# A Perceiver layer on one core: query, key and value weights split inside the walk, three second products in three passes, a residual on GpSimd

## What is computed

```python
x = x + xattn(layernorm(x), ctx)          # x 128 x 512, ctx 12544 x 512, 16 heads
# k' = relu(k Wkf'), v: kv = sum over ctx of k' v, ksum = sum of k';  out = (q' kv) / (q' ksum) @ Wo'
x = x + attn(layernorm(x))
# q, k, v = rms(x) @ w_qkv.T;  y = sigmoid(rms q) * cumsum(exp(rms k) * v) / cumsum(exp(rms k))
# u, g = split(y @ w_swiglu.T)            # 2048 each
# attn(x) = x + (u * silu(g)) @ w_out.T   # the "x +" here adds the normed input once more
x = x + ffn(layernorm(x))                 # 2 experts, top-1, hidden 2048, squared leaky relu
```

## Time and profile before

| | |
|---|---|
| median of 3 runs | 875.67 us (875.64 to 875.98) |
| the profiled execution's own time | 875.99 us |
| its span in the profile | 874.2 us |
| from one full tile to the next, and from one short tile to the next | 7.42 us (693.65 to 701.07), 6.12 us (726.83 to 732.95) |
| granted TensorE clock | 1.00 over the whole span |
| busy: TensorE, VectorE, ScalarE, GpSimd | 861.8, 668.1, 563.6, 363.1 us |

### The profile page before, as it was taken

How to read it: one execution, slowest core, us unless ns; L and a number is a source line. 1 busy time by engine, 2 the same in 40 slices (tenths; PEclk the granted TensorE clock), 3 DMA queues, 4 the chain that set the end, 5 groups by cost and what they waited for, 6 DMA issues and landing times.

```text
span 874.2 us, 14769 instructions
## 1 busy us (share of the span) xinstructions
PE 861.8 (99%) x4728; PEld 742.4 (85%) x4728; DVE 668.1 (76%) x1048; ACT 563.6 (64%) x988; POOL 363.1 (42%) x208
## 2 busy tenths in 40 slices
PE   8999999999999999999999999999999999899998
PEld 6888888888888888888888888888888888778788
DVE  5777777777777777777777777777777788889586
ACT  5666666666666666666666666666666666754453
POOL 2654454445555444555554444445555433000000
PEclk9999999999999999999999999999999999999999
DMA  7212121121101010101010101001010000659740
GB/s 267 95 52 88 58 72 72 61 83 50 70 24 48 24 48 24 48 24 48 24 48 24 48 24 42 30 28 44 24 48 25 25 1 28 241 202 354 250 157 13
DMA packets 18504, 64.15 MB, mean 73 GB/s; under 512 B 2224, under 2 KB 2992, under 8 KB 18096
## 3 DMA queue, kind: packets, MB, share of 16 engines
q1 hardware_dynamic: 17760, 63.58, 20.6%
q10 hardware_dynamic: 720, 0.25, 0.1%
HBM read 63.56 MB, written 0.26 MB: 73 GB/s over the span
## 4 chain that ended last, share of the span: by engine, by line
PE 95%; ACT 2%; DVE 1%; DMA 1%; issue 0%; SPq 0%; DVEq 0%; ACTq 0%
PE kv_ps L798 11%; PE f_ps L785 10%; PE v_bank L701 10%; PE k_bank L701 10%; PE v_bank L702 10%; PE k_bank L702 10%; PE v_bank L703 10%; PE k_bank L703 10%; PE kv_ps L1016 3%; PE kv_ps L1035 2%; ACT w_hi L594 1%; PE k_bank L881 1%; PE v_bank L881 1%; PE k_bank L887 1%; PE v_bank L893 1%; PE v_bank L887 1%
## 5 line engine op out<-in xcount | busy, mean ns | idle before, releaser
L412 POOL TENSOR_TENSOR ksum_acc<-ksum_acc,kf 128x1024 f32<-128x1024 f32 x96 | 230.9, 2405 | 190.0 <-DVE kf L1137 190.0
L500 ACT ACTIVATE fb<-f_ps 128x256 f32<-128x256 f32 x392 | 149.6, 382 | 172.5 <-PE f_ps L785 165.2
L1130 DVE TENSOR_TENSOR kf<-f_ps,fb 128x256 f32<-128x256 f32 x392 | 165.5, 423 | 109.0 <-ACT fb L500 103.5
L405 POOL TENSOR_TENSOR ctx_lo<-ctx_raw,ctx_hi 128x512 fp32r<-128x512 f32 x92 | 119.5, 1299 | 170.1 <-ACT ctx_hi L475 170.1
L785 PEld LDWEIGHTS f_ps<-bd,keys 128*128 128x128 f32 x784 | 146.3, 188 | 33.8 <-issue 1.3
L785 PE MATMUL f_ps<-bd,keys 128*128 128x256 f32 x784 | 155.9, 281 | 1.3 <-DVE kf L1130 1.3
L701 PE MATMUL k_bank<-ctx_hi,wk_lo 128*128 128x512 f32 (+1 forms) x392 | 152.5, 389 | 0.8 <-DVE ctx_lo L1209 0.7
L701 PE MATMUL v_bank<-wv_hi,ctx_lo 128*128 128x512 f32 x388 | 153.2, 395 | 0.0
L483 ACT ACTIVATE keys<-k_bank,bias_cols 64x512 fp32r<-64x512 f32 (+1 forms) x194 | 131.0, 675 | 34.4 <-PE k_bank L703 31.9
L702 PE MATMUL v_bank<-wv_lo,ctx_hi 128*128 128x512 f32 x388 | 152.6, 393 | 0.0
L702 PE MATMUL k_bank<-ctx_lo,wk_hi 128*128 128x512 f32 (+1 forms) x392 | 152.2, 388 | 0.0
(11 more groups left out here) (214 smaller groups left out, 935.4 us busy)
## 6 DMA issues: line engine op xcount, KB each, us to landing
ctx_raw<-in_ctx SPq DMA_DIRECT2D x46, 512.0 KB, 3.3
early<-in_stream SPq DMA_DIRECT2D x14, 1024.0 KB, 4.9
raw<-in_stream SPq DMA_DIRECT2D x10, 1024.0 KB, 5.3
early<-in_stream SPq DMA_DIRECT2D x14, 512.0 KB, 4.3
early<-in_ctx SPq DMA_DIRECT2D x2, 512.0 KB, 6.3
early<-in_wv SPq DMA_DIRECT2D x1, 1024.0 KB, 8.7
early<-in_wq SPq DMA_DIRECT2D x1, 1024.0 KB, 10.7
w_o<-in_wo SPq DMA_DIRECT2D x1, 1024.0 KB, 5.3
```

Of the source, the lines that this page charges most:

```text
L405: pool.tensor_tensor(ctx_lo[:, s, :, cols], raw[:, :, t % 2 * P:(t % 2 + 1) * P], ctx_hi[:, s, :, cols].bitcast(f32), ALU.subtract).then_i ...
L412: pool.tensor_tensor(ksum_acc[:, :].rearrange("p (j f) -> p j f", f=P), ksum_acc[:, :].rearrange("p (j f) -> p j f", f=P), kf[:, t % 2, :, ...
L500: act.activation(fb[:, i % 2, :, :], f_ps[i % 2][:, :].rearrange("p (j x f) -> p j x f", j=2, x=2) [:, :, 1, :], ACT.Copy).then_inc(fb_rea ...
L1130: dve.tensor_tensor(kf[:, t % 2, 2 * i:2 * i + 2, :], f_ps[i % 2][:, :].rearrange("p (j x f) -> p j x f", j=2, x=2)[:, :, 0, :], fb[:, i % ...
```

## The change

Four things. The parts of GK, GQ and GV are made in the last twelve tiles before `tile_last`: ScalarE copies a quarter of a group (128 x 512) at the end of each tile, and VectorE subtracts the quarter before at the start of the next one, ahead of share 0. For that their high parts get places of their own (`w_lo[0..2]`), four groups instead of seven are loaded in the walk, and the loads behind it begin with group 4. Second, GD[0], GD[1] and GD[2] are made in three passes, with their weights and hidden values split. Third, the residual with the normed input is made by GpSimd, ahead of the gated layer. Fourth, the lists of splits behind the walk are shifted accordingly.

```diff
-NG_EARLY = 7
+NG_EARLY = 4
+SLOTS_EARLY = 7
...
-SPLIT = [GK, GQ, GV, GG[0], GU[0], GG[1], GU[1], GG[2], GU[2], GG[3], GU[3], *GF_[0:6], GP[3],
+BEFORE = [GK, GQ, GV]
+SPLIT = [GG[0], GU[0], GG[1], GU[1], GG[2], GD[0], GU[2], GG[3], GU[3], GD[1], GD[2], *GF_[0:6], GP[3],
          GF_[6], GP[4], GF_[7], *GP[5:8]]
...
+DOWNS = [0, 1, 2, *range(DFF // D + FIRST, 3 * DFF // D)]
+
+
+def slot_of(g):
+    return (g + 3) % RAWS
...
         def high(g):
-            return w_hi[SPLIT.index(g) % HIS]
+            return w_lo[g] if g in BEFORE else w_hi[SPLIT.index(g) % HIS]
...
@@ block.sync
             sp.wait_ge(f_done, JOBS * NT)
-            load_group(7)
-            load_group(8)
+            load_group(4)
+            load_group(5)
 
             sp.wait_ge(kv_done, NT + 1)
             sp.wait_ge(ksumT_done, 1)
-            load_group(9)
-            load_group(10)
-
-            for g in range(RAWS, NG):
-                sp.wait_ge(group_used, g - RAWS + 1)
+            load_group(6)
+            load_group(7)
+
+            for g in range(8, NG):
+
+                sp.wait_ge(group_used, min(g - 7, 3) if g < 14 else g - 10)
                 load_group(g)
...
@@ block.gpsimd
+            z1 = gate[:, 0, :]
+            pool.wait_ge(act_ready, 4)
+            pool.tensor_scalar(z1, x1[:, :], stat[:, 6:7], stat[:, 8:9], ALU.subtract, ALU.mult).then_inc(z1_ready, 1)
+            pool.wait_ge(z1_ready, 1)
+            pool.tensor_tensor(x1[:, :], x1[:, :], z1, ALU.add).then_inc(x1_ready, 1)
             rstd(3, 8, 1)
...
@@ block.scalar
+            def qkv_high(i):
+                g, k = BEFORE[i // KC], i % KC
+                act.activation(high(g)[:, k, :], raw(g)[:, k, :], ACT.Copy).then_inc(qkv_hi_ready, 1)
+
+            def period(c, s, splits=TILES, keys=CHUNK, pieces=0):
                 n = TILES * c
                 for t in range(TILES):
                     tile(n + t, t, keys=((c + 1, 1 - s, t, k_bank, keys),),
                          splits=((2 * c + 4 + t // 2, s, t),) if t < splits else ())
+                    if pieces:
+                        qkv_high(TILES * (pieces - 1) + t)
...
-            period(LAST - 3, 1)
-            period(LAST - 2, 0, splits=LAST_TILES)
-            period(LAST - 1, 1, splits=0, keys=HALF)
+            act.wait_ge(early_loaded, 16 * NPIECE)
+            period(LAST - 3, 1, pieces=1)
+            period(LAST - 2, 0, splits=LAST_TILES, pieces=2)
+            period(LAST - 1, 1, splits=0, keys=HALF, pieces=3)
...
             act.wait_ge(f_done, JOBS * NT)
-            for g in (2, 3, 4):
-                weight_high(g)
+            weight_high(GU[0])
+            weight_high(GG[1])
 
             act.wait_ge(kv_done, NT + 1)
-            for g in (5, 6):
-                weight_high(g)
+            weight_high(GU[1])
...
-                t = hid_hi[n % 2][:, :, :] if n >= DFF // D + FIRST else hid_T2[n % 2]
+                t = hid_hi[n % 2][:, :, :] if n in DOWNS else hid_T2[n % 2]
...
@@ block.tensor
                     group(GG[n], k_ps[n % 2], 0 if n else 3)
                     if n == 2:
-                        hidden_down(0, GD[0], True, False)
+                        hidden_down_split(0, GD[0], True, False)
                     group(GU[n], v_ps[n % 2])
                 if 1 <= n <= nd:
                     hidden_turn(n - 1)
-                if n >= 3:
-                    hidden_down(n - 2, GD[n - 2], False, n == nd + 1)
+                if n in (3, 4):
+                    hidden_down_split(n - 2, GD[n - 2], False, False)
+            hidden_down(nd - 1, GD[nd - 1], False, True)
...
@@ block.vector
+            def qkv_low(i):
+                g, k = BEFORE[i // KC], i % KC
+                dve.wait_ge(qkv_hi_ready, i + 1)
+                dve.tensor_tensor(low(g)[:, k, :], raw(g)[:, k, :], high(g)[:, k, :].bitcast(f32), ALU.subtract)\
+                   .then_inc(qkv_lo_ready, 1)
+
+            def period(c, s, keys=CHUNK, pieces=0):
                 n = TILES * c
                 for t in range(TILES):
+                    i = TILES * (pieces - 1) + t
+                    if pieces and i:
+                        qkv_low(i - 1)
                     tile(n + t, t, keys=((c + 1, 1 - s, t, k_bank, keys),))
...
-            period(LAST - 3, 1)
-            period(LAST - 2, 0)
-            period(LAST - 1, 1, keys=HALF)
+            period(LAST - 3, 1, pieces=1)
+            period(LAST - 2, 0, pieces=2)
+            period(LAST - 1, 1, keys=HALF, pieces=3)
+            qkv_low(3 * KC - 1)
...
+            before_gate = ((7, 10), (10, 13), (13, 16), (18, 20))
+            before_up = ((), (), (16, 18), (20, 21))
+            dve.wait_ge(x1_ready, 1)
             for n in range(nd):
+                low_pieces(*before_gate[n])
 
                 dve.wait_ge(gateg_ready, n + 1)
                 e = gate[:, n % 2, :]
                 link(dve.tensor_tensor(e, k_ps[n % 2], e, ALU.mult))
+                if before_up[n]:
+                    low_pieces(*before_up[n])
                 dve.wait_ge(group_used, GU[n] + 1)
                 dve.tensor_tensor(hid[:, n % 2, :], v_ps[n % 2], e, ALU.mult).then_inc(hid_ready, 1)
-                low_pieces(14 + 4 * n - 2 * (n == 3), 18 + 4 * n - 2 * (n >= 2))
-                if n == 2:
-
-                    dve.wait_ge(rstd_ready, 2)
-                    link(dve.tensor_scalar(eq[:, :], x1[:, :], stat[:, 6:7], stat[:, 8:9], ALU.subtract, ALU.mult))
-                    link(dve.tensor_tensor(x1[:, :], x1[:, :], eq[:, :], ALU.add))
+                if n:
+                    hidden_low(n - 1)
+            low_pieces(21, 26)
```

More of the change, by code:

```diff
@@ L66, in perceiver_kernel @@
         scope.close()
-        w_lo = [sb(f"w_lo{i}", [P, KC, D], f32r) for i in range(NG_EARLY)]
+        w_lo = [sb(f"w_lo{i}", [P, KC, D], f32r) for i in range(SLOTS_EARLY)]
         x_sb = sb("x_sb", [P, D])
@@ L536, in tile_last @@
                 features_share(n, 3, False)
-            def period(c, s, splits=TILES, keys=CHUNK):
+            def qkv_high(i):
+                g, k = BEFORE[i // KC], i % KC
+                act.activation(high(g)[:, k, :], raw(g)[:, k, :], ACT.Copy).then_inc(qkv_hi_ready, 1)
+            def period(c, s, splits=TILES, keys=CHUNK, pieces=0):
                 n = TILES * c
@@ L671, in _ @@
                     act.wait_ge(hid_ready, n - 1)
+                if n == 0:
+                    act.wait_ge(x1_ready, 1)
                 act.activation(gate[:, n % 2, :], k_ps[n % 2], ACT.Sigmoid).then_inc(gateg_ready, 1)
+                for g in ((GU[2], GG[3]), (), GD[2:3], GF_[1:2])[n]:
+                    weight_high(g)
                 if n:
                     hidden_turned(n - 1)
-                for g in (GU[3:4], GF_[0:1], GF_[1:2], GF_[2:4])[n]:
+                for g in ((), (GU[3], GD[1]), GF_[0:1], ())[n]:
                     weight_high(g)
             hidden_turned(nd - 1)
+            for g in GF_[2:4]:
+                weight_high(g)
             turned_high(4)
@@ L872, in wait_low, with wait_high @@
             def wait_low(g, h):
-                pe.wait_ge(w_lo_ready, PIECES.index((g, h)) + 1)
+                if g in BEFORE:
+                    pe.wait_ge(qkv_lo_ready, KC * BEFORE.index(g) + 2 * h + 2)
+                else:
+                    pe.wait_ge(w_lo_ready, PIECES.index((g, h)) + 1)
+            def wait_high(g):
+                if g in BEFORE:
+                    pe.wait_ge(qkv_hi_ready, KC * BEFORE.index(g) + KC)
+                else:
+                    pe.wait_ge(w_hi_ready, 2 * SPLIT.index(g) + 2)
             def hi_hi(g, ps, x, cols, start, turned=0):
-                pe.wait_ge(w_hi_ready, 2 * SPLIT.index(g) + 2)
+                wait_high(g)
                 for k in range(KC):
@@ L1020, in hidden_down, with hidden_down_split @@
                 last.then_inc(group_used, 1)
-            def hidden_down_split(n, g, last_one):
-                i = n - DFF // D - FIRST
+            def hidden_down_split(n, g, first, last_one):
+                i = DOWNS.index(n)
                 pe.wait_ge(hidT_ready, n + 1)
-                pe.wait_ge(w_hi_ready, 2 * SPLIT.index(g) + 2)
+                wait_high(g)
                 for bs in ([[0], [1]] if last_one else [[0, 1]]):
@@ L1035, in hidden_down_split @@
                                 last = pe.matmul(half_ps[b], x[n % 2][:, k, :], w[:, k, b * D // 2:(b + 1) * D // 2],
-                                                 start=False, stop=last_one and x is hid_lo and k == KC - 1)
+                                                 start=first and x is hid_hi and not low_w and k == 0,
+                                                 stop=last_one and x is hid_lo and k == KC - 1)
                     if bs == [0]:
@@ L1041, in _ @@
             nd = DFF // D
-            for n in range(nd + 2):
+            for n in range(nd + 1):
                 if n < nd:
@@ L1188, in tile_last @@
                     masked_features(n, t)
```

(18 more changed lines are left out.)

59 lines of the change are left out of this document (27 added, 32 removed).

## The result

| | before | after |
|---|---|---|
| median, 7 runs each | 875.90 us (875.46 to 877.27) | 878.86 us (878.51 to 879.97) |
| profiled execution, its span | 875.99, 874.2 us | 878.68, 876.2 us |

The changed kernel is slower: ratio 1.0031, interval 1.0021 to 1.0041. That is 2.96 us where 2.0 were forecast. Some executions of either kernel show a mean granted clock of 0.998 instead of 1.00 and take 1 to 2 us longer; the medians include them.

A forecast was written before the change was run, and what follows sets the result against it. TensorE, busy 99% of the span, was taken to bound the kernel. The terms, -0.50 - 1.86 + 0.1 + 4.3 = +2.0 us, put the median at 877.7 us, with the range 874.7 to 878.9.

The forecast's parts named there:

- Quarters on VectorE in the walk: In short tiles, the subtraction ahead of share 0 waits for GpSimd's feature sum and delays share 1; 4.3 us lost.
- the next instruction starts 0.08 before its record ends: After the held quarter on VectorE, share 0 starts 0.08 us before the quarter's recorded end, at K + 2.92.
- Pricing a short tile by the lateness of share 1: Share 1 starts 0.93 us late, TensorE's job 3 and the next keys with it, so each such tile pays 0.93.
- the full hold: Main case: the walk's subtraction stands still until GpSimd's sum is done, less 0.14; 876.5 to 878.7 us, chance 0.62.
- The first (not held, 873.4): The walk's subtraction finds VectorE idle and isn't held up, so only the gains stay; 873.4 us, chance 0.14.
- The second, half speed: Subtraction and GpSimd's sum share the port at half speed, quarter 1.2 us, 1.4 lost; 874.8 us, chance 0.17.
- A hold that breaks early: The walk's subtraction is held only for a part of GpSimd's sum; up to 876.4 us, within the half-speed chance of 0.17.
- The third: Longer hold costs seven full tiles 0.1 to 0.2 each, residual on GpSimd meets VectorE's products for 0.5; 879.2, chance 0.07.
- Backlog: Behind the walk, fewer half groups on ScalarE let the first copy of turned_high(2) start earlier; 0.50 us gained.
- Three passes: In the gated layer, three second products on TensorE take 2.84 us each instead of 3.46; 1.86 us gained.
- ScalarE's quarters: In the walk, each quarter copy of about 0.5 us fits ScalarE's idle time ahead of share 0; nothing lost.
- The residual: Two GpSimd instructions near 772 end by about 774.5 and could hold one VectorE product 0 to 0.2; 0.1 lost.

The follow-up runs named there:

- the first two runs: Changed kernel with the walk's VectorE subtractions replaced by one-operand bn_stats, 873.67 us; changed kernel with GpSimd's feature sum in short tiles cut to 8 columns, 873.89 us.
- The version with full tiles: Changed kernel with the twelve quarters moved one period earlier into the last twelve full tiles, on VectorE ahead of share 3; 873.49 us, ratio 0.9965.

## Why the prediction was right in sign and short by one

**Quarters on VectorE in the walk: forecast 4.3, measured 5.05. The mechanism was right, the size off.** The hold was as forecast: the quarter got through 0.14 before GpSimd's end and ended 0.55 after it (forecast 0.5), and took 1.97 (near 2.0). Full tiles kept their length (708.40 - 700.99 = 7.41). The step that failed is "the next instruction starts 0.08 before its record ends": share 0 starts 0.03 after the quarter's end (725.85 against 725.82), so shares 0 and 1 came at K + 3.03 and K + 4.50, where 2.92 and 4.39 were forecast. That is 0.11 in each of five tiles, 0.55 of the missing 0.75. By the starts of the keys before and after, the five tiles lose 0.83, 1.05, 1.06, 1.05 and 1.06, together 5.05 (to job 3 at 742.25 against 737.51, plus 0.31 by which this execution's walk ran earlier from its start-up). Most of the rest, about 0.1, is in the first of them. The forecast said 0.6 for the first and 0.93 for the others. Pricing a short tile by the lateness of share 1 was sound: share 1 is 4.50 - 3.46 = 1.04 late and the tile 1.06 longer, over the path that the prediction named. The idle stands elsewhere than I wrote: not 0.9 ahead of job 3, but 0.31 ahead of job 2 and 0.26 ahead of job 3. Job 2 needs share 0, which the prediction had end at K + 3.34; in a short tile job 2 is due at 730.41 - 727.37 = K + 3.04, so by its own numbers job 2 had to wait. I had looked at job 2 in full tiles only.

The range held by 0.04 (878.86, with 878.9 as its end), and the 876.5 to 878.7 that I gave to the full hold itself did not. The mechanism is shown; that the number fell inside is luck.

**Rivals.** The first (not held, 873.4) is what the first two runs make by hand, 873.67 and 873.89, so its time was right and its condition false. The second, half speed, is out: at half speed 0.68 becomes 1.36 at most, and it took 1.97. A hold that breaks early is out as well, since the quarter ends where GpSimd's end puts it. The third needed a hold longer than in the rows, which no run shows.

The Trainium skill's rule that speaks against this place (SBUF — State Buffer, "Who interferes with whom") is borne out on both sides. With two SBUF inputs the instruction is held, 1.97 against 0.68. The page also says that a VectorE instruction with at most one SBUF input, outside certain modes, does not contend; the run with one operand agrees, with 0.69 beside GpSimd's sum. One SBUF tile is not safe in every case, though: the `tensor_scalar` at 754.09 reads only `den` and still ended with GpSimd's instruction. No run here takes that case apart.

**Backlog: 0.50 forecast, 0.50 measured**: the copy starts 0.48 behind the transposes instead of 0.98. **Three passes: 1.86 forecast, 1.87 measured** from the first product of the gated layer to the end of the last (782.89 to 818.99 against 778.65 to 816.62); no low part came late, and each takes 2.86 rather than 2.84. **ScalarE's quarters** cost nothing, as forecast. **The residual: 0.1 forecast, 0 seen in the trace.** Its instructions are longer than the nearest row let expect (2.08 and 1.50 against 1.05), but end at 779.93 and were asked for at about 784: a wrong size under a cover that was large enough. Behind the gated layer another 0.31 is gained that I had not forecast. It stands at one place of the chain, between the end of the last product and VectorE's first addition behind it: 0.45 before (816.62 to 817.07) and 0.10 after (818.99 to 819.09). The chain has there before:

```profile
809.70 6.92 PE kv_ps L1016 x32
...
817.07 0.43 DVE x L1306
```

and after:

```profile
819.09 0.43 DVE x L1350
```

The versions with plain second products and with the residual back on VectorE have about 0.10 too, so it is neither of these; what it is stays open.

**The sum.** In the span: 5.05 - 0.31 - (0.50 + 1.87 + 0.31) = 2.1, and the two spans are 2.0 apart. The rest of the 2.96 has two parts. The profiled execution of the changed kernel was among its shorter ones: at a clock of 1.00 the medians of the spans are 876.4 and 873.9 (the latter from the executions of before beside the first runs), 2.5 apart. And 0.5 lies outside the span (2.3 against 1.8 in the median). My sum had no term for it; what makes it stays open. The version with full tiles has 2.0 outside, so it goes with the program in some way that is not the number of semaphores.

## What to carry to other kernels

Before you add a VectorE instruction with two operands in SBUF, look at what GpSimd does at that moment: beside a 2.4 us sum, 0.68 became 1.97, and the same twelve instructions placed in VectorE's idle time turned 3.0 lost into 2.4 gained. Follow what waits for what around the whole loop, across engines, and take each small step between two instructions from a pair like it: 0.03 after the end instead of 0.08 before it was most of what the main term missed. Take a change apart before you judge it: here one misplaced instruction hid two gains.
